# Last layer of a four-layer graph network: one-hots built by ScalarE in groups of four, segment product in two short-float passes for two tiles of three

## The reference, cut to what matters

```python
h = jnp.maximum(_layernorm(x, axis=-1), 0.0)
x = x + _L3_gnn_ref(h, edge_index_t, 625, W, b)

def _L3_gnn_ref(x, edge_index, num_local_nodes, W, b):
    src, tgt = edge_index[:, 0], edge_index[:, 1]
    x_ij = jnp.concatenate([x[src], x[tgt]], axis=1)      # 10625 x 1024
    m_ij = jax.nn.relu(x_ij @ W.T + b)                    # 10625 x 512
    return jax.ops.segment_sum(m_ij, src, num_segments=num_local_nodes)
```

## Time and profile before

| what | us |
|---|---|
| median of 3 runs | 1161.28 (1159.26 to 1161.47) |
| profiled execution: span from the first to the last instruction | 1157.3 |
| median of the runs less that span (launch and end) | 4.0 |
| layer four's loop in it, from 1041.76 to 1150.99 | 109.2 |
| PE busy in the loop | 108.3 |
| DVE busy in the loop | 99.3 |
| ACT busy in the loop | 65.0 |
| POOL busy in the loop | 78.4 |

### The profile page before, as it was taken

One profiled execution on the slowest core, in us unless ns is written; L12 is line 12 of the kernel. 1 busy time (PEld: TensorE's weight loads), 2 busy tenths in 40 slices (PEclk: granted clock), 3 DMA queues, 4 the chain that ended last, 5 costly groups with the idle time before them and its releaser, 6 DMA issues. The chain is left out here.

```text
span 1157.3 us, 15307 instructions
## 1 busy us (share of the span) xinstructions
PE 1077.4 (93%) x4358; PEld 588.5 (51%) x4358; DVE 857.3 (74%) x2016; ACT 557.9 (48%) x978; POOL 503.1 (43%) x434
## 2 busy tenths in 40 slices
PE   3679978899999989899999999999999999999997
PEld 1124323344557454655565555555556557446665
DVE  5996677769755153688788788878878867849997
ACT  0221321310332221477777777777777744215664
POOL 0000112243333430668876666666666200027774
PEclk9878999999999999899999999999999999999999
DMA  7986998657211005695554454444455010026665
GB/s 283 359 329 234 356 406 299 231 187 241 74 50 46 14 14 194 135 258 111 111 112 92 101 96 97 97 98 98 93 99 92 1 46 31 9 87 200 205 205 177
DMA packets 60182, 172.65 MB, mean 149 GB/s; under 512 B 12645, under 2 KB 13189, under 8 KB 52552
## 3 DMA queue, kind: packets, MB, share of 16 engines
q0 software_dynamic: 31536, 72.01, 26.7%
q1 hardware_dynamic: 28568, 99.66, 23.3%
HBM read 159.65 MB, written 11.98 MB: 148 GB/s over the span
## 5 line engine op out<-in xcount | busy, mean ns | idle before, releaser
L1635 PE MATMUL PS<-wide,hidT 128*128 128x512 f32 x672 | 302.1, 592 | 0.0
L689 POOL DMA_INDIRECT rec_scratch<-rec_src,slot_row x84 | 100.3, 1195 | 260.1 <-DMA rec_scratch<-rec_src,slot_row 206.3
L1635 PEld LDWEIGHTS PS<-wide,hidT 128*128 128x128 f32 x672 | 128.6, 191 | 122.8 <-issue 120.5
L1569 ACT ACTIVATE wide<-PS 128x512 f32<-128x512 f32 x168 | 100.3, 597 | 99.9 <-PE PS L1619 63.5
L1453 POOL DMA_INDIRECT pair_sum<-table_j,counts_rec x84 | 136.4, 1624 | 26.9 <-issue 25.3
L1772 POOL DMA_INDIRECT u_space<-table_j,wide x87 | 85.3, 980 | 108.6 <-DMA table_j<-agg_space 81.7
L1445 POOL DMA_INDIRECT pair_sum<-table_i,counts_rec x84 | 89.5, 1065 | 97.1 <-PE PS L1619 59.7
L1574 ACT ACTIVATE wide<-wide,two 128x512 f32<-128x512 f32 x168 | 120.9, 719 | 6.2 <-DVE wide L1504 6.2
L1504 DVE SCALAR_TENSOR_TENSOR wide<-wide 128x512 f32<-128x512 f32 x168 | 116.4, 693 | 5.8
L1579 ACT ACTIVATE wide<-wide 128x512 f32<-128x512 f32 x168 | 105.8, 630 | 5.3
L1462 POOL DMA_INDIRECT rec_scratch<-rec_src,slot_row x84 | 87.6, 1043 | 40.6 <-issue 22.2
(11 more groups left out here) (321 smaller groups left out, 1838.1 us busy)
## 6 DMA issues: line engine op xcount, KB each, us to landing
pieces<-basis_rows SPq DMA_DIRECT2D x56, 1024.0 KB, 7.3
ring<-basis_low SPq DMA_DIRECT2D x30, 256.0 KB, 6.4
w_scratch<-pieces SPq DMA_DIRECT2D x112, 32.0 KB
counts_rec<-rec_scratch SPq DMA_DIRECT2D x1, 2856.0 KB, 9.8
rec_scratch<-rec_src,slot_row POOLq DMA_INDIRECT x168, 2.3
root<-L_gnn_root SPq DMA_DIRECT2D x2, 1024.0 KB, 6.4
rows_in<-in_rows_in SPq DMA_DIRECT2D x2, 1024.0 KB, 15.1
w_rel<-w_scratch SPq DMA_DIRECT2D x1, 2048.0 KB
```

The lines of the kernel that those rows point to most:

```text
L689: nc.gpsimd.indirect_dma_start(out=rec3_dram, out_offset=bass.IndirectOffsetOnAxis(ap=slot_row[:, 1, t:t + 1], axis=0), in_=rec, in_offset ...
L1569: nc.scalar.activation(grow[l][:, t % 2, :], PS[:, bank, :], ACT.Exp).then_inc(sem(f"exp{l}"), 1)
L1635: m = nc.tensor.matmul(o, hidT[:, t % 2, k * P:(k + 1) * P], w2[:, k, :], start=False, stop=(k == KT - 1), skip_group_check=True)
```

## The change

Five things are changed, all in the last block.

1. `in_two` is now t % 3 != 0: 58 of the 87 tiles go through `sum_hi`/`sum_lo` and two short passes (before 43), 29 through one full-float product (before 44). `sum_hi` and `sum_lo` have rings of 4 tiles instead of 3, `relu5` of 2 instead of 3.
2. DVE no longer makes the one-hots: neither the first eight nor one per tile.
3. ACT makes them, four tiles at once (`one_hots`): four `Abs` activations of 128 x 128 give |source - column| into `hot_far`, then, after a wait for these, one `Relu` of 128 x 512 gives max(0, 1 - that). A wait for this Relu's own end follows.
4. ACT does the first two groups behind layer three's last activation and ahead of the first `estimate`, then group j+2 at t = 4j+2, between ReLU 4j+1 and ReLU 4j+2, for j up to 19.
5. PE's `turn` counts groups instead of tiles; DVE does a last `low_sum` for tile 86.

```diff
-            GOT5, HOT5, PAIR5, SPLIT5, TURN_GROUP = 8, 16, 6, 3, 4
+            GOT5, HOT5, PAIR5, SPLIT5, RELU5, TURN_GROUP, HOTS_AHEAD = 8, 16, 6, 4, 2, 4, 2
-            in_two = lambda t: t % 2 == 1
+            in_two = lambda t: t % 3 != 0
+            n_two = lambda t: t - (t + 2) // 3
...
+            hot_far = w3[:, 0, :].rearrange("p (g n) -> p g n", g=TURN_GROUP)
...
-                def one_hot(t):
-                    if t >= HOT5:
-                        dve.wait_ge(sem("sum_mm5"), t - HOT5 + 1)
-                    nc.vector.tensor_scalar(is_src5[:, t % HOT5, :], slot_of_col[:], rec5[:, t, 1:2], None,
-                                            ALU.is_equal).then_inc(sem("is_src5"), 1)
...
-                dve.wait_ge(sem("rec5_in"), 16)
-                for t in range(2 * TURN_GROUP):
-                    one_hot(t)
...
                 for t in range(NS):
                     add_pair(t)
-                    if t + 2 * TURN_GROUP < SC:
-                        one_hot(t + 2 * TURN_GROUP)
                     if t and in_two(t - 1):
                         low_sum(t - 1)
-                assert not in_two(NS - 1)
+                if in_two(NS - 1):
+                    low_sum(NS - 1)
...
+                def one_hots(j):
+
+                    at = TURN_GROUP * j % HOT5
+                    if TURN_GROUP * j >= HOT5:
+                        act.wait_ge(sem("sum_mm5"), TURN_GROUP * (j + 1) - HOT5)
+                    for g in range(TURN_GROUP):
+                        t = TURN_GROUP * j + g
+                        nc.scalar.activation(hot_far[:, g, :], slot_of_col[:], ACT.Abs, bias=rec5[:, t, 1:2],
+                                             scale=-1.0).then_inc(sem("hot_far"), 1)
+                    act.wait_ge(sem("hot_far"), TURN_GROUP * (j + 1))
+                    nc.scalar.activation(is_src5[:, at:at + TURN_GROUP, :], hot_far, ACT.Relu, bias=1.0, scale=-1.0).then_inc(sem("is_src5"), 1)
+                    act.wait_ge(sem("is_src5"), j + 1)
...
+                act.wait_ge(sem("rec5_in"), 16)
+                for j in range(HOTS_AHEAD):
+                    one_hots(j)
                 estimate(0, 0)
...
                 for t in range(NS):
                     if t % TURN_GROUP == 1 and t // TURN_GROUP + 1 < N_TURN:
                         turned(t // TURN_GROUP + 1)
+                    if t % TURN_GROUP == 2 and t // TURN_GROUP + HOTS_AHEAD < N_TURN:
+                        one_hots(t // TURN_GROUP + HOTS_AHEAD)
                     act.wait_ge(sem("pair_sum5"), t + 1)
...
-                    pe.wait_ge(sem("is_src5"), TURN_GROUP * (j + 1))
+                    pe.wait_ge(sem("is_src5"), j + 1)
```

More of the change, by code:

```diff
@@ L1718, in gnn_stack @@
         with p45:
-            GOT5, HOT5, PAIR5, SPLIT5, TURN_GROUP = 8, 16, 6, 3, 4
+            GOT5, HOT5, PAIR5, SPLIT5, RELU5, TURN_GROUP, HOTS_AHEAD = 8, 16, 6, 4, 2, 4, 2
             LAG5 = 4
-            in_two = lambda t: t % 2 == 1
+            in_two = lambda t: t % 3 != 0
+            n_two = lambda t: t - (t + 2) // 3
+            at_two = [t for t in range(NS) if in_two(t)]
+            at_one = [t for t in range(NS) if not in_two(t)]
+            assert all(at_two[n_two(t)] == t for t in at_two)
             l3w = counts_rec[:, 0:2 * KT * D].rearrange("p (k o) -> p k o", k=2 * KT)
@@ L1729, in gnn_stack @@
             pair5 = wide[:, 0:PAIR5 * D].rearrange("p (b o) -> p b o", b=PAIR5)
-            relu5 = u_space[:, GOT5 * D:(GOT5 + PAIR5 // 2) * D].rearrange("p (b o) -> p b o", b=PAIR5 // 2)
+            relu5 = u_space[:, GOT5 * D:(GOT5 + RELU5) * D].rearrange("p (b o) -> p b o", b=RELU5)
             sum_hi = sb("sum_hi", [P, SPLIT5, D], F32R, p45)
@@ L1854, in add_pair @@
                         if in_two(t - PAIR5):
-                            dve.wait_ge(sem("sum_lo"), (t - PAIR5) // 2 + 1)
+                            dve.wait_ge(sem("sum_lo"), n_two(t - PAIR5) + 1)
                     nc.vector.tensor_tensor(pair5[:, t % PAIR5, :], PS[:, own_bank(t), :], got5[:, t % GOT5, :],
@@ L1891, in low_sum @@
                 def low_sum(t):
-                    n = t // 2
+                    n = n_two(t)
                     dve.wait_ge(sem("relu5"), t + 1)
                     if n >= SPLIT5:
-                        dve.wait_ge(sem("sum_mm5"), t - 2 * SPLIT5 + 1)
+                        dve.wait_ge(sem("sum_mm5"), at_two[n - SPLIT5] + 1)
                     nc.vector.scalar_tensor_tensor(sum_lo[:, n % SPLIT5, :], pair5[:, t % PAIR5, :], 0.0, sum_hi[:, n % SPLIT5, :].bitcast(F32),
@@ L1972, in _ @@
                     if in_two(t):
[L1973 to L1976, removed]
-                    else:
-                        nc.scalar.activation(relu5[:, t // 2 % (PAIR5 // 2), :], pair5[:, t % PAIR5, :], ACT.Relu).then_inc(sem("relu5"), 1)
+                        n = n_two(t)
+                        if n >= SPLIT5:
+                            act.wait_ge(sem("sum_mm5"), at_two[n - SPLIT5] + 1)
+                            act.wait_ge(sem("sum_lo"), n - SPLIT5 + 1)
+                        nc.scalar.activation(sum_hi[:, n % SPLIT5, :], pair5[:, t % PAIR5, :], ACT.Relu).then_inc(sem("relu5"), 1)
+                    else:
+                        n = t // 3
+                        if n >= RELU5:
+                            act.wait_ge(sem("sum_mm5"), at_one[n - RELU5] + 1)
+                        nc.scalar.activation(relu5[:, n % RELU5, :], pair5[:, t % PAIR5, :], ACT.Relu).then_inc(sem("relu5"), 1)
             @block.tensor
@@ L2050, in seg_sum @@
                     if in_two(t):
-                        pe.wait_ge(sem("sum_lo"), t // 2 + 1)
+                        pe.wait_ge(sem("sum_lo"), n_two(t) + 1)
                         for part in (sum_hi, sum_lo):
-                            m = nc.tensor.matmul(at, is_src5[:, t % HOT5, :], part[:, t // 2 % SPLIT5, :], start=False, stop=False, skip_group_check=True)
+                            m = nc.tensor.matmul(at, is_src5[:, t % HOT5, :], part[:, n_two(t) % SPLIT5, :], start=False, stop=False, skip_group_check=True)
                     else:
                         pe.wait_ge(sem("relu5"), t + 1)
-                        m = nc.tensor.matmul(at, is_src5[:, t % HOT5, :].bitcast(F32), relu5[:, t // 2 % (PAIR5 // 2), :],
+                        m = nc.tensor.matmul(at, is_src5[:, t % HOT5, :].bitcast(F32), relu5[:, t // 3 % RELU5, :],
                                              start=False, stop=False, skip_group_check=True)
```

## The result

The changed kernel takes 1171.13 us (median of 4 runs, 1167.57 to 1173.10), the kernel before 1161.38 (4 runs): ratio 1.0084, 95% interval 1.0059 to 1.0109, or +9.8 us (+6.9 to +12.7). The forecast was 1174.8 with a range of 1165 to 1180: slower, as said, by three quarters of the size. One execution of a later kernel, the one without one-hots in the loop, took 6215 us where its eleven others took 1160 to 1169, and no figure here counts it.

What follows compares the result with a forecast made beforehand. PE was taken to bound the loop before, with gathers close behind, and the ACT-DVE handover after. Terms +1.9 ahead of the loop, +11.8 in it and -0.2 at its end gave 1161.3 + 13.5 = 1174.8 us, range 1165 to 1180.

Steps and rivals of the forecast that it cites:

- PE's saving: Loop of layer four: fifteen tiles go from 0.86 to 0.47 us on PE, 5.9 us in all, not all visible.
- the handover: Loop: DVE can run only one tile ahead of ACT, so each waits for the other; +11.8 us, ReLU 1 to 81.
- The one-hot block: ACT, in and ahead of the loop: one group of one-hots takes 2.06 us, low end 1.44, high end 2.38.
- the rival of cheap one-hots: Loop: groups of one-hots at the low end, gathers set the pace, 1162; up to 1.66 us each, 1166; chance 0.12.
- three kinds of group: Loop: groups of four tiles differ by which tile is the one-pass one, taking 5.80, 5.62 and 5.14 us.
- From ReLU 81 to 86: End of the loop, without one-hots: five tiles at PE's 1.17 take 5.8 us against 6.05, -0.2.
- Ahead of the loop: Before layer four's loop: two groups of one-hots on ACT delay the first estimate, nothing absorbs it; +1.9 us.
- PE's clock: Rival, in the loop: PE's waits make its clock fall to 1.2 GHz, +95 us, 1256; chance 0.03.
- Signs that failed: Loop trace, if right: PE's idle time grows by 15 us or more, groups of four take 5.1 to 5.8.
- faster: Rival, in the loop: ACT's idle time takes the one-hots, long gathers shorten, end up to 2.9 us earlier, 1158.4; chance 0.05.
- no overlap: Rival, in the loop: the Abs do not overlap, or the chain collects jitter; 1178 to 1182; chance 0.10.

Runs made afterwards that it cites:

- split only: Against the kernel before: two short passes for two tiles of three, DVE still making every one-hot; 1161.12 us, ratio 1.0002.
- both repairs: Against the changed kernel: DVE makes the first eight one-hots long ahead and does low_sum(t-2) behind add(t); 1162.21 us, ratio 1.0004.
- DVE two ahead: Against the changed kernel: DVE does low_sum(t-2) instead of low_sum(t-1) behind add(t); 1163.64 us, ratio 1.0016.

## Why the prediction was right, and where its sizes were off

- **PE's saving is made and not seen.** Right. Even without the handover's loss it would not be seen, because of the gathers, as the prediction said: split only shows nothing, and with both repairs nine gathers fewer make the loop 4.9 us shorter. The saving itself was put too high, at 5.9 us against 4.7.
- **The one-hot block.** I took 2.06 us, it is 1.96: four Abs in 1.27 instead of 1.33, and the Relu is 0.63, the low one of the two values I had set out. From ReLU 4j+1 to ReLU 4j+2 it is therefore 2.50, not 2.60. For an input in SBUF the rival of cheap one-hots named 0.09 us, but the earlier trace rows has that only for the bias; the copy out of PSUM in the earlier trace rows is 0.06 shorter than the ReLU. The Trainium skill's formula (ScalarE: Activation LUTs, section What ACT_TABLE_LOAD costs), with 1.94 for the block, was nearer than my reading of the rows: it gives 387 ns for an Abs, and the profile after shows 388.
- **The handover.** Right in its mechanism and its constants. With 2.50 the three kinds of group come to 5.70, 5.52 and 5.04; measured 5.69, 5.49 and 5.01. ReLU 1 to ReLU 81 took 1157.69 - 1049.98 = 107.7 us, forecast 110.1. Of the 2.4 us between, 20 x 0.10 are the block's size.
- **From ReLU 81 to 86** I reckoned with PE's pace, 5.8; it took 5.1. In the profile DVE goes through these tiles without a pause, five adds and three low parts, so its pace held and not PE's. The block's size (2.0 us over 20 groups), this tail (0.7) and about 0.4 of handover steps slightly shorter than read make the loop +8.4 instead of the forecast +11.6. The block is the largest term of the 3.7 us by which the forecast was too high.
- **Ahead of the loop** the delay is 1.61 us, forecast 1.93; 0.2 by the block's size, 0.1 because the first Abs overlaps the last activation before it.
- **PE's clock.** I looked for it in the loop, where it stayed at 1.00, and held waits of 2.4 us harmless because the earlier trace rows showed one with the clock up. That was one observation of something that goes either way: waits of 2.40 and 2.67 us are seen here both with the dip and without it. It is worth 1.7 us in an execution that has it. The dip ahead of the loop was missing in the forecast, where it would have made the sum still larger: a gap that hid behind terms put too high.
- **Signs that failed.** PE's idle time in the loop was to grow by 15 us or more; it grew from 0.9 to 6.8, by 5.9. Busy time is not what PE needs: the ends of matmuls are modelled, and the same 432 matmuls, busy for 110.81 us here, are busy for 103.31 of 104.10 us in the loop of the kernel with both repairs and nine gathers fewer, where PE is the chain. And the shortest groups took 5.01 us, a little below the 5.1 named.
- **Cheap one-hots, faster, no overlap:** none came. The long gathers of the earlier trace rows do not hang on DVE's one-hots, as the rival "faster" supposed: of 87 gathers six or seven are still over 1.05 us with DVE two ahead, without one-hots in the loop and with both repairs, where DVE makes none in the loop. The second low part was the reason why the whole change costs more than its parts; the forecast had this in its three kinds of group without saying so.

## What to carry to other kernels

Where two in-order engines pass tiles back and forth, ask how many tiles the first can run ahead. With one tile of slack a block of foreign work on the second engine costs little while the group with it is about as long as the pace of the engine that bounds the loop (+1.2 us in all with the old split), more when another step joins the chain (+8.4), and from there on it is paid in full (+23.2 for 23.2), however idle both engines look. Here moving one dependent instruction a tile later in the program got it back without any added work. Before shortening the engine that bounds a loop, read the pace of the next one: here a gather every 1.286 us, slower even than PE's 1.23 and hidden only by a lead of eight buffers, so that nothing of PE's saving could show. And put work into an engine's idle time only where nobody waits for what stands behind it.

## What was not expected of the hardware

The granted clock of PE dipped for some microseconds ahead of the loop in five of fourteen profiles, behind waits of 2.40 to 2.67 us, and stayed up behind waits of the same length in the others; eight matmuls then took 5.1 to 5.3 us instead of 3.60. And the gathers' pace is not a constant of their number: from gather 8 to gather 86 it was 100.28 us before, but 97.74 in the kernel with only the one-hots on ACT, in whose profile none of the long gathers of the earlier trace rows occurs. What makes them long stays open.
